# Moving half of a depthwise convolution from VectorE to diagonal matrix products on TensorE, and taking C from the joint projection, in the front part of a state-space and mixture-of-experts kernel

## The chip, the cores and the metric

The kernel runs on one core of one Trainium2 chip. The metric is the device time of one execution, in microseconds (us); lower is better.

## The reference, cut to what matters

```
xn = layernorm(x)                                   # x: 2 x 2048 tokens x 512 channels
xc = depthwise causal convolution of xn, 4 taps per channel, + conv_b
x_conv = silu(xc)
proj = x_conv @ xproj_w.T                           # 512 -> 128 (dt_in) + 16 (B_in) + 16 (C_in)
delta = softplus(dt_in @ dtproj_w.T + dtproj_b)
h_t = exp(delta * A) * h_(t-1) + delta * B_in * x_conv    # scan over time, 16 states per channel
y = sum over the states of h * C_in + xn * D
g = silu(mixture_of_experts(xn))                    # 8 experts, top 2, capacity 1024 each
out = x + y * g
```

## The kernel before, in words

The program has three parts that follow one another: `front`, `main_loop` (the experts' products with the scan woven in) and `tail`. The change touches `front` alone.

`front` works in 8 chunks of 512 tokens (`NCH`, `CH`), with the 512 channels as 4 tiles of 128 partitions (`KT`, written kt). Its first half normalises the chunks, turns them to channels by tokens (`xnT`, each chunk with 3 tokens of the chunk before as a halo) and computes the router's logits. Its second half, which the change is about, does for each chunk ch:

- VectorE, `convolve` (L492 to L507): four taps on each of four channel tiles, from `xnT` into `conv`: one `tensor_scalar` (L502, first tap and bias) and three `scalar_tensor_tensor` (L506) for a tile, 16 instructions a chunk. It waits until the silu of the chunk before has read `conv`.
- ScalarE, `silu` (L349 to L354): four activations from `conv` back into `xnT`.
- TensorE, `project` (L277 to L285): for each kt one product for the 128 dt rows (L283, to `pX` bank 0) and one for the 16 B rows (L284, to bank 1).
- ScalarE, `copy_projection` (L356 to L363): copies dt into `dtin` and B into `brows`; `store_b` sends B to memory.
- TensorE, `widen_dt` (L287 to L293): four products into the four banks of `pT`. Then `c_by_token` (L295 to L303): C by tokens, 4 token blocks times 4 kt, 16 products of 16 columns each with the tokens as stationary operand, into `pC`.
- ScalarE, `softplus` (L370 to L388): reads `pT` into `z`, then Abs, Exp (two halves each) and, after waits for stores and for `u`, Ln. `copy_ct` (L365 to L368) then copies C into `ct`.
- VectorE, `soft` (L574 to L592) and GpSimd (L439): the rest of softplus; L592 writes delta. GpSimd (L445) multiplies delta by the silu's result to `u`. GpSimd also scatters the router's table by 64 indirect DMAs (L434): 24 ahead of chunk 0, then 7 a chunk.
- SyncE stores delta and u and reads the router's table back (L213), for which VectorE waits (L604) ahead of its last `soft`.

Nothing schedules this: each engine runs its own program in the order in which it is written, and semaphores do the rest. ScalarE's loop is, for chunk ch: `copy_projection(ch)`, `silu(ch + 1)`, `store_b(ch)`, `softplus(ch)`, `copy_ct(ch)`. VectorE's is `convolve(ch + 2)`, `soft(ch)`. TensorE's is `project`, `widen_dt`, `c_by_token`. Ahead of its loop VectorE does `convolve(0)` and then some 60 small instructions of the router, at whose end the semaphore `placed` is raised; `pC` holds the router's counts until then. The float32 products are recorded as two instructions each, so counts of matmuls in the trace are twice those of the code.

Of the kernel before, what the change touches and what calls it, by code (L numbers as in the profile page):

```python
# [29 lines left out]
ALU = mybir.AluOpType  # L30
ACT = mybir.ActivationFunctionType
AX = mybir.AxisListType.X
ds = bass.ds

P = 128
B, T, D = 2, 2048, 512
S = B * T
KT = D // P
N = 16
TAPS = 4  # L40
R = 128
E, HID = 8, 2048
CAP = 2 * S // E
CH = 512
NCH = S // CH
CPB = T // CH
TPC = CH // P
# [5 lines left out]
HALO = TAPS - 1  # L53
# [4 lines left out]
C_TAP, C_CONVB, C_DTB, C_ALOG = 0, TAPS, TAPS + 1, TAPS + 2  # L58
# [33 lines left out]
def apart(eng, sem):  # L92

    eng.sem_inc(sem, 1)


def front(nc, a, dr, keep):

    with ExitStack() as ctx:
        sb, psum, sems = memory(nc, ctx)  # L100
        ident, tri, ones = sb("f_ident", [P, P]), sb("f_tri", [P, P]), sb("f_ones", [P, P])
# [15 lines left out]
        lgT = sb("lgT_sb", [E, CH])  # L117
        logits = sb("logits_sb", [P, NT, E])
        zeros, warm = sb("zeros_sb", [P, 512]), sb("f_warm", [P, 1])
        conv = sb("conv_sb", [P, KT, CH])  # L120
        dtin = sb("dtin_sb", [P, CH])
        brows = sb("brows_sb", [N, CH])
        za, z = sb("za_sb", [P, KT, CH]), sb("z_sb", [P, KT, CH])
        ln = sb("ln_sb", [P, KT, CH])
        back = sb("back_sb", [P, KT, CH])
# [14 lines left out]
        pC = psum("pC", [P, 2, CH])  # L140

        s_ = sems("f_", """early consts x_in0 x_in1 xn_out0 xn_out1 cleared stats moments power normed xT xT_copied
            lgT lgT_copied lg lg_copied route shifted exped masks counted placed defaults scattered table
            indexed zeroed halo taps silu proj dtin b_rows b_out dt dt_read absz expz
            lnz rounded dropped dropped_dve soft delta u_done delta_out u_out neg_a ct ct_copied
            pe_at act_at dve_at sp_at pool_at""")

# [75 lines left out]
        @block.tensor  # L223
        def _(pe):
            for name, credits in (("xT", KT + 1), ("lg", 1), ("proj", 1), ("dt", 1)):
                pe.sem_inc(s_[name], credits)
            pe.wait_ge(s_["early"], 16 * len(early))

            def turn(ch, u, i):

                pe.wait_ge(s_["normed"], ch + 3)
                for kt in range(KT):

                    pe.wait_ge(s_["xT_copied"], KT * ch + kt + 1)
                    for j in range(TPC):
                        mm = pe.transpose(pT[:, kt, j * P:(j + 1) * P], xn[:, u, j, kt * P:(kt + 1) * P], ident[:])
                    mm.then_inc(s_["xT"], 1)

            def logits_T(ch):

                pe.wait_ge(s_["xT_copied"], KT * ch + 2 * KT)
                pe.wait_ge(s_["lgT_copied"], ch + 1)
                for kt in range(KT):
                    mm = pe.matmul(pX[0:E, 0, :], wg[:, kt, :], xnT[:, ds(ch, 1), kt, HALO:], start=(kt == 0), stop=(kt == KT - 1))
                mm.then_inc(s_["lgT"], 1)

            def turn_logits(ch):
                pe.wait_ge(s_["lgT_copied"], ch + 2)

                pe.wait_ge(s_["lg_copied"], ch + 1)  # L250
                apart(pe, s_["pe_at"])
                for j in range(TPC):
                    mm = pe.transpose(pX[:, 1, j * E:(j + 1) * E], lgT[:, j * P:(j + 1) * P], ident[0:E, 0:E])
                mm.then_inc(s_["lg"], 1)

            turn(0, 0, 0)
            with pe.Fori(0, NCH // 2 - 1) as i:
                for u in range(2):
                    logits_T(2 * i + u)
                    turn(2 * i + u + 1, 1 - u, i)  # L260
                    turn_logits(2 * i + u)
            logits_T(NCH - 2)
            turn(NCH - 1, 1, 0)
            turn_logits(NCH - 2)
            logits_T(NCH - 1)
            turn_logits(NCH - 1)

            pe.wait_ge(s_["consts"], 16 * len(consts))

            pe.wait_ge(s_["masks"], 1)  # L270
            pe.wait_ge(s_["lg_copied"], NCH + 1)
            for s in range(2):
                for k, w in enumerate((tri, ones)):
                    mm = pe.matmul(pC[:, s, k * NT * E:(k + 1) * NT * E], w[:], mask[s][:].rearrange("p t e -> p (t e)"), start=True, stop=True)
            mm.then_inc(s_["counted"], 1)

            def project(ch):  # L277

                pe.wait_ge(s_["b_rows"], ch + 1)
                for kt in range(KT):  # L280
                    pe.wait_ge(s_["silu"], KT * ch + kt + 2)
                    xs = xnT[:, ds(ch, 1), kt, HALO:]
                    pe.matmul(pX[:, 0, :], xprojT[:, kt, 0:R], xs, start=(kt == 0), stop=(kt == KT - 1))  # L283
                    mm = pe.matmul(pX[0:N, 1, :], xprojT[:, kt, R:R + N], xs, start=(kt == 0), stop=(kt == KT - 1))  # L284
                mm.then_inc(s_["proj"], 1)  # L285

            def widen_dt(ch):  # L287

                pe.wait_ge(s_["dtin"], ch + 1)
                for kt in range(KT):  # L290

                    pe.wait_ge(s_["dt_read"], KT * ch + kt + 1)
                    pe.matmul(pT[:, kt, :], dtprojT[:, kt * P:(kt + 1) * P], dtin[:], start=True, stop=True).then_inc(s_["dt"], 1)  # L293

            def c_by_token(ch):  # L295

                pe.wait_ge(s_["placed"], 1)
                pe.wait_ge(s_["ct_copied"], ch + 1)
                for tb in range(TPC):
                    for kt in range(KT):  # L300
                        xs = xnT[:, ch, kt, HALO + tb * P:HALO + (tb + 1) * P]
                        mm = pe.matmul(pC[:, 0, tb * N:(tb + 1) * N], xs, xprojT[:, kt, R + N:], start=(kt == 0), stop=(kt == KT - 1))
                mm.then_inc(s_["ct"], 1)  # L303

            for ch in range(NCH):
                project(ch)
                widen_dt(ch)
                c_by_token(ch)

        @block.scalar  # L310
        def _(act):
            for name, credits in (("xT_copied", KT), ("lgT_copied", 1), ("lg_copied", 1), ("silu", 1), ("b_rows", 1),
                                  ("dt_read", KT), ("b_out", 16), ("ct_copied", 1)):
                act.sem_inc(s_[name], credits)

# [32 lines left out]

            def silu(ch):  # L349

                for kt in range(KT):
                    act.wait_ge(s_["taps"], KT * (TAPS * ch + HALO) + kt + 1)
                    apart(act, s_["act_at"])
                    act.activation(xnT[:, ds(ch, 1), kt, HALO:], conv[:, kt, :].unsqueeze(1), ACT.Silu).then_inc(s_["silu"], 1)  # L354

            def copy_projection(ch):  # L356
                act.wait_ge(s_["proj"], ch + 2)

                act.wait_ge(s_["dt"], KT * ch + 1)
                act.activation(dtin[:], pX[:, 0, :], ACT.Copy).then_inc(s_["dtin"], 1)  # L360

                act.wait_ge(s_["b_out"], 16 * ch + 16)
                act.activation(brows[:], pX[0:N, 1, :], ACT.Copy).then_inc(s_["b_rows"], 1)  # L363

            def copy_ct(ch):  # L365
                act.wait_ge(s_["ct"], ch + 1)
                apart(act, s_["act_at"])
                act.activation(keep["ct"][:, ds(TPC * ch, TPC), :], pC[:, 0, 0:TPC * N].rearrange("p (j n) -> p j n", n=N), ACT.Copy).then_inc(s_["ct_copied"], 1)  # L368

            def softplus(ch):  # L370

# [17 lines left out]

            def store_b(ch):  # L390

                act.wait_ge(s_["b_rows"], ch + 2)
                act.dma_start(dr.b[ds(ch, 1)].rearrange("o n t -> n (o t)"), brows[:]).then_inc(s_["b_out"], 16)

            silu(0)
            with act.Fori(0, NCH - 1) as ch:
# [51 lines left out]
        def _(dve):  # L448
# [43 lines left out]
            def convolve(ch):  # L492

                dve.wait_ge(s_["silu"], KT * ch + 1)
                for k in range(TAPS):
                    for kt in range(KT):
                        x = xnT[:, ds(ch, 1), kt, HALO - k:HALO - k + CH]
                        c = conv[:, kt, :].unsqueeze(1)
                        tap = chan[:, kt, C_TAP + HALO - k:C_TAP + HALO - k + 1]
                        if k == 0:  # L500

                            op = dve.tensor_scalar(c, x, tap, chan[:, kt, C_CONVB:C_CONVB + 1], ALU.mult, ALU.add)  # L502
                        else:

                            dve.wait_ge(s_["taps"], KT * (TAPS * ch + k - 1) + kt + 1)
                            op = dve.scalar_tensor_tensor(out=c, in0=x, scalar=tap, in1=c, op0=ALU.mult, op1=ALU.add)  # L506
                        op.then_inc(s_["taps"], 1)  # L507

            dve.wait_ge(s_["halo"], 1)
            convolve(0)  # L510
            chain = [0]

            def link(op):
# [775 lines left out]
```

## Time and profile before

| what | us |
|---|---|
| median of 3 runs | 2161.86 |
| lowest and highest run | 2161.03, 2163.65 |
| the profiled execution, its own time | 2175.82 |
| its span | 2174.0 |
| `front` in it (to the first DMA of `main_loop`) | 0 to 307.5 |
| from there until TensorE is done | 307.5 to about 2110 |
| `tail` | about 2110 to 2174.0 |

Times in the rows below are of the profiled execution and count from its span's start. In the timelines a row is a group of like instructions that follow one another: start, time from the first start to the last end, engine, line, operation, output and inputs, count, and in brackets the idle time of the engine ahead of the group and what ended it. A busy TensorE row contains the time that its matmuls take at the clock then granted, which is one of two levels, 1.2 and 2.4 GHz.

### The profile page before, as it was taken

To read this page: it belongs to the slowest core of one execution; us is meant where nothing else is said; L and a number is where in the kernel's file an instruction comes from. 1 tells how busy PE (TensorE), PEld (TensorE's weight loads), DVE (VectorE), ACT (ScalarE), POOL (GpSimd) and SP (SyncE) were. 2 spreads that over 40 slices of the span, in tenths; PEclk is the share of its full clock that TensorE was granted. 3 is DMA by queue.
4 is the path that set the end of the run, shared out by engine and by line. 5 is a ranking of instruction groups with operands and counts; after the bars stand their busy time and mean duration, and the time that the engine had idled before them with its cause. 6 is when DMAs were issued, how large, how long until landed. Compare 5 with 4: busy or idle time off the path is not lost. (4 is left out here: it accounts for less than half of the span.)

```text
span 2174.0 us, 30995 instructions
## 1 busy us (share of the span) xinstructions
PE 1884.3 (87%) x9160; PEld 1477.4 (68%) x9160; DVE 1909.0 (88%) x2038; ACT 1215.3 (56%) x1778; POOL 1383.0 (64%) x606
## 2 busy tenths in 40 slices
PE   6667829999999999999999999999999999999500
PEld 3223317888778788878887888788877887788400
DVE  6777938988998889898989998999899989988599
ACT  3265737656656665656565655665656565655121
POOL 1167748657866676667567756675667566766444
PEclk9877758999999999999999999999999999999855
DMA  9623344214421451235124412441244124321597
GB/s 290 238 44 77 118 187 97 83 58 140 96 80 63 136 117 63 68 128 116 63 68 133 116 58 68 147 102 58 73 142 102 58 79 152 89 75 62 133 320 248
DMA packets 89192, 246.96 MB, mean 114 GB/s; under 512 B 13296, under 2 KB 14320, under 8 KB 77808
## 3 DMA queue, kind: packets, MB, share of 16 engines
q1 hardware_dynamic: 70640, 207.30, 28.2%
q0 software_dynamic: 18176, 37.83, 9.6%
q8 instruction: 72, 1.18, 0.2%
q14 instruction: 48, 0.39, 0.1%
q10 hardware_dynamic: 256, 0.26, 0.1%
HBM read 173.66 MB, written 71.70 MB: 113 GB/s over the span
## 5 line engine op out<-in xcount | busy, mean ns | idle before, releaser
L988 POOL TENSOR_TENSOR ub_sb<-u_sb,brow_sb 128x1024 f32<-128x1024 f32 x256 | 639.7, 2499 | 410.2 <-DVE a_sb L1078 406.3
L1078 DVE TENSOR_TENSOR_SCAN a_sb<-a_sb,state,ub_sb 128x512 f32<-128x512 f32 x512 | 884.5, 1767 | 11.6 <-issue 7.7
L738 PE MATMUL pm<-xTh,w1l 128*128 128x512 f32 x1024 | 424.2, 414 | 11.8 <-DVE xTl L1026 5.3
L738 PE MATMUL pm<-w2h,hl 128*128 128x512 f32 x1024 | 423.9, 414 | 0.0
L740 PE MATMUL pm<-xTh,w1h 128*128 128x512 f32 x1024 | 402.8, 393 | 0.0
L740 PE MATMUL pm<-w2h,hh 128*128 128x512 f32 x1024 | 402.5, 393 | 0.0
L739 PE MATMUL pm<-w2l,hh 128*128 128x512 f32 x1024 | 399.5, 390 | 0.0
L739 PE MATMUL pm<-xTl,w1h 128*128 128x512 f32 x1024 | 399.3, 390 | 0.0
L1049 DVE SCALAR_TENSOR_TENSOR s_acc<-pt,ct_keep,s_acc 128x512 f32<-128x512 f32 x480 | 352.1, 734 | 27.1 <-PE pt L768 26.2
L888 ACT ACTIVATE a_sb<-delta_sb,neg_a_keep 128x512 f32<-128x512 f32 x512 | 330.1, 713 | 6.5
L768 PE MATMUL pt<-m_ident,a_sb 128*128 128x128 f32 x2048 | 308.2, 273 | 25.5 <-DVE a_sb L1078 17.8
L768 PEld LDWEIGHTS pt<-m_ident,a_sb 128*128 128x128 f32 x2048 | 250.6, 139 | 100.4 <-issue 24.0
L911 ACT ACTIVATE hh<-pm,b_keep 128x512 fp32r<-128x512 f32 x256 | 176.1, 688 | 176.3 <-PE pm L740 172.1
L1058 DVE TENSOR_TENSOR hl<-pm,hh 128x512 fp32r<-128x512 f32 x256 | 174.4, 681 | 73.4 <-ACT pm L912 69.4
L738 PEld LDWEIGHTS pm<-xTh,w1l 128*128 128x128 f32 x1024 | 193.6, 189 | 44.4 <-issue 8.3
L740 PEld LDWEIGHTS pm<-xTh,w1h 128*128 128x128 f32 x1024 | 192.8, 188 | 44.0
L740 PEld LDWEIGHTS pm<-w2h,hh 128*128 128x128 f32 x1024 | 192.6, 188 | 43.5
L739 PEld LDWEIGHTS pm<-xTl,w1h 128*128 128x128 f32 x1024 | 194.1, 190 | 32.8
L739 PEld LDWEIGHTS pm<-w2l,hh 128*128 128x128 f32 x1024 | 194.0, 189 | 32.8
L738 PEld LDWEIGHTS pm<-w2h,hl 128*128 128x128 f32 x1024 | 193.4, 189 | 30.8
L977 POOL TENSOR_TENSOR w2l<-w_raw,w2h 128x2048 fp32r<-128x2048 f32 x32 | 176.9, 5527 | 55.2 <-ACT w2h L850 55.2
L1066 DVE SCALAR_TENSOR_TENSOR part<-pm,gate_keep,part 128x512 f32<-128x512 f32 x256 | 186.8, 730 | 27.8 <-PE pm L740 27.8
(130 smaller groups left out, 2139.9 us busy)
## 6 DMA issues: line engine op xcount, KB each, us to landing
w_raw<-in_w SPq DMA_DIRECT2D x64, 1024.0 KB, 5.0
brow_sb<-b_chunks SPq DMA_DIRECT2D x128, 256.0 KB, 3.5
moe_rows<-zeros_sb SPq DMA_DIRECT2D x5, 2048.0 KB, 16.8
xin_sb<-in_x SPq DMA_DIRECT2D x8, 1024.0 KB, 6.3
xn_rows<-xn_sb SPq DMA_DIRECT2D x8, 1024.0 KB, 8.5
delta_chunks<-ln_sb SPq DMA_DIRECT2D x8, 1024.0 KB
u_chunks<-u_now_sb SPq DMA_DIRECT2D x16, 512.0 KB, 4.7
delta_sb<-delta_chunks SPq DMA_DIRECT2D x8, 1024.0 KB, 7.8
```

What stands on the lines that cost most here:

```text
L738: pe.matmul(out, sl, mh, start=start, stop=False)
L739: pe.matmul(out, sh, ml, start=False, stop=False)
L740: return pe.matmul(out, sh, mh, start=False, stop=stop)
L768: mm = pe.transpose(pt[:, bank(s, last), kt * P:(kt + 1) * P], abuf[:, m, kt, tb * P:(tb + 1) * P], ident[:])
L888: op = act.activation(abuf[:, m, kt, :], delta[:, kt, :], ACT.Exp, scale=keep["neg_a"][:].rearrange("p n k -> p (n k)")[:, ds(col, 1)])
L911: act.activation(hh[:, g, j, :], pm[:, j, :], ACT.Gelu, bias=bias)
L977: pool.tensor_tensor(lo[:].rearrange("p k f -> p (k f)"), raw[:], hi[:].rearrange("p k f -> p (k f)").bitcast(F32), ALU.subtract).then_inc ...
L988: pool.tensor_tensor(ub[:, h], u[:, 2 * h:2 * h + 2, :], brow[:, m % 2:m % 2 + 1, :].to_broadcast([P, 2, CH]), ALU.mult).then_inc(s_["bmul ...
L1049: dve.scalar_tensor_tensor(out=acc, in0=h, scalar=c, in1=acc, op0=ALU.mult, op1=ALU.add).then_inc(s_["summed"], 1)
L1058: dve.tensor_tensor(hl[:, g, j, :], pm[:, j, :], hh[:, g, j, :].bitcast(F32), ALU.subtract).then_inc(s_["h_free"], 1)
L1066: dve.scalar_tensor_tensor(out=part[:, t, :], in0=pm[:, t % 4, :], scalar=gate, in1=part[:, t, :], op0=ALU.mult, op1=ALU.add).then_inc(s_[ ...
L1078: op = dve.tensor_tensor_scan(abuf[:, m, 2 * h + k, :], abuf[:, m, 2 * h + k, :], ub[:, h, k, :], state[:, ds(col, 1)], ALU.mult, ALU.add)
```

## The change

Half of the channel tiles (kt 2 and 3) are convolved by TensorE. VectorE builds once, between `convolve(0)` and the router's instructions, 8 diagonal matrices of 128 by 128 from the taps (`diag`). For each chunk TensorE's new `convolve` accumulates four products per tile (a diagonal matrix by `xnT` shifted by one token a tap) in `pC`; silu reads `pC` with the bias of the convolution. C comes with B: the product of L284 now has 32 output rows, `copy_projection` copies all 32 rows, and `turn_c` turns them by four small transposes into bank 1 of `pX`, from which `copy_ct` picks C. As the transposes share that bank with the B and C rows of the next projection, `project` now also waits for `ct_copied`. TensorE's unrolled loop over chunks becomes a loop with register addresses; in it the convolution of chunk ch + 1 stands ahead of the projection of chunk ch.

```diff
-        conv = sb("conv_sb", [P, KT, CH])
+        conv = sb("conv_sb", [P, KT // 2, CH])
+        diag = sb("diag_sb", [P, KT // 2, TAPS, P])
...
-        brows = sb("brows_sb", [N, CH])
+        bcrows = sb("bcrows_sb", [2 * N, CH])
...
+            def convolve(ch):
+
+                pe.wait_ge(s_["silu"], KT * ch + 1)
+                for i, kt in enumerate(range(KT // 2, KT)):
+                    for k in range(TAPS):
+                        mm = pe.matmul(pC[:, i, :], diag[:, i, k, :], xnT[:, ds(ch, 1), kt, HALO - k:HALO - k + CH],
+                                       start=(k == 0), stop=(k == TAPS - 1))
+                    mm.then_inc(s_["conv_pe"], 1)
+
             def project(ch):
 
-                pe.wait_ge(s_["b_rows"], ch + 1)
+                pe.wait_ge(s_["bc_rows"], ch + 1)
+                pe.wait_ge(s_["ct_copied"], ch + 1)
                 for kt in range(KT):
                     pe.wait_ge(s_["silu"], KT * ch + kt + 2)
                     xs = xnT[:, ds(ch, 1), kt, HALO:]
                     pe.matmul(pX[:, 0, :], xprojT[:, kt, 0:R], xs, start=(kt == 0), stop=(kt == KT - 1))
-                    mm = pe.matmul(pX[0:N, 1, :], xprojT[:, kt, R:R + N], xs, start=(kt == 0), stop=(kt == KT - 1))
+                    mm = pe.matmul(pX[0:2 * N, 1, :], xprojT[:, kt, R:], xs, start=(kt == 0), stop=(kt == KT - 1))
                 mm.then_inc(s_["proj"], 1)
...
-            def c_by_token(ch):
-
-                pe.wait_ge(s_["placed"], 1)
-                pe.wait_ge(s_["ct_copied"], ch + 1)
+            def turn_c(ch):
+
+                pe.wait_ge(s_["bc_rows"], ch + 2)
+                apart(pe, s_["pe_at"])
                 for tb in range(TPC):
-                    for kt in range(KT):
-                        xs = xnT[:, ch, kt, HALO + tb * P:HALO + (tb + 1) * P]
-                        mm = pe.matmul(pC[:, 0, tb * N:(tb + 1) * N], xs, xprojT[:, kt, R + N:], start=(kt == 0), stop=(kt == KT - 1))
+                    mm = pe.transpose(pX[:, 1, tb * 2 * N:(tb + 1) * 2 * N], bcrows[:, tb * P:(tb + 1) * P], ident[0:2 * N, 0:2 * N])
                 mm.then_inc(s_["ct"], 1)
 
-            for ch in range(NCH):
+            pe.wait_ge(s_["placed"], 1)
+            pe.wait_ge(s_["diag"], 1)
+            pe.wait_ge(s_["halo"], 1)
+            convolve(0)
+            with pe.Fori(0, NCH - 1) as ch:
+                convolve(ch + 1)
                 project(ch)
                 widen_dt(ch)
-                c_by_token(ch)
+                turn_c(ch)
+            project(NCH - 1)
+            widen_dt(NCH - 1)
+            turn_c(NCH - 1)
...
             def silu(ch):
 
-                for kt in range(KT):
-                    act.wait_ge(s_["taps"], KT * (TAPS * ch + HALO) + kt + 1)
+                for kt in range(KT // 2):
+                    act.wait_ge(s_["taps"], KT // 2 * (TAPS * ch + HALO) + kt + 1)
                     apart(act, s_["act_at"])
                     act.activation(xnT[:, ds(ch, 1), kt, HALO:], conv[:, kt, :].unsqueeze(1), ACT.Silu).then_inc(s_["silu"], 1)
+                for i, kt in enumerate(range(KT // 2, KT)):
+                    act.wait_ge(s_["conv_pe"], KT // 2 * ch + i + 1)
+                    apart(act, s_["act_at"])
+                    act.activation(xnT[:, ds(ch, 1), kt, HALO:], pC[:, i, :].unsqueeze(1), ACT.Silu,
+                                   bias=chan[:, kt, C_CONVB:C_CONVB + 1]).then_inc(s_["silu"], 1)
...
                 for k in range(TAPS):
-                    for kt in range(KT):
+                    for kt in range(KT // 2):
...
             convolve(0)
+            for i in range(KT // 2):
+                for k in range(TAPS):
+                    tap = chan[:, KT // 2 + i, C_TAP + HALO - k:C_TAP + HALO - k + 1]
+                    op = dve.tensor_scalar(diag[:, i, k, :], ident[:], tap, None, ALU.mult)
+            op.then_inc(s_["diag"], 1)
```

TensorE of the kernel before, from the widening of one chunk (L293) over its C (L302) to the projection of the next (L283, L284):

```order
L293 MATMUL pT<-dtin_sb,dtprojT_sb 128x512 [waits f_dt_read,f_dtin]
L293 MATMUL pT<-dtin_sb,dtprojT_sb 128x512 [waits f_dt_read] x3
L302 MATMUL pC<-xprojT_sb,xnT_sb 128x16 [waits f_ct_copied,f_placed]
L302 MATMUL pC<-xprojT_sb,xnT_sb 128x16 x15
L283 MATMUL pX<-xnT_sb,xprojT_sb 128x512 [waits f_silu,f_b_rows]
```

TensorE of the changed kernel, in its loop (its lines are numbered anew: L283 is the convolution, L294 and L295 the projection), from the last product of the convolution of chunk ch + 1 into the projection of chunk ch:

```order
L283 ISA
L283 MATMUL pC<-xnT_sb,diag_sb 128x512
L292 ISA [waits f_ct_copied,f_bc_rows]
L294 ISA [waits f_silu]
L294 MATMUL pX<-xnT_sb,xprojT_sb 128x512
L295 MATMUL pX<-xnT_sb,xprojT_sb 32x512
```

The wait for `ct_copied` has moved from C's product to the head of the projection, and the convolution of the next chunk stands ahead of that wait. Where C's 16 products stood, the changed kernel has, up to the end of the loop's body (L304 is the widening, L311 the turning):

```order
L303 REGISTER_ALU [waits f_dtin]
L304 MATMUL pT<-dtin_sb,dtprojT_sb 128x512 [waits f_dt_read] x4
L308 REGISTER_ALU
L311 MATMUL pX<-f_ident,bcrows_sb 128x32 [waits f_bc_rows]
L311 MATMUL pX<-f_ident,bcrows_sb 128x32 x3
L318 REGISTER_ALU
L318 COMPARE_AND_BRANCH
```

Four transposes stand in the place of the 16 products, and they wait for the copied rows.

## Rows read from the trace of the kernel before

**Rows 1.** Busy time by stage: front, main loop; length, engines, PEclk, DMA share, GB/s
```profile
0.00:307.50 307.50, 200.76 (x680) 88.23 (x680) 224.73 (x347) 153.80 (x250) 149.79 (x108) 0.81 0.48 149
307.50:2110.00 1802.50, 1683.53 (x8480) 1389.16 (x8480) 1624.42 (x1647) 1050.46 (x1518) 1205.43 (x490) 0.97 0.35 102
```
**Rows 2.** Timeline of VectorE, one round of its loop (L502 to L592)
```profile
193.46 5.83 DVE L502 TENSOR_SCALAR conv_sb<-xnT_sb,chan_sb 128x512 f32 x4
199.20 8.02 DVE L506 SCALAR_TENSOR_TENSOR conv_sb<-xnT_sb,chan_sb,conv_sb 128x512 f32<-128x512 f32 x12
207.15 1.33 DVE L580 TENSOR_SCALAR back_sb<-za_sb 128x1024 f32<-128x1024 f32 x2
...
214.22 2.36 DVE L592 TENSOR_TENSOR ln_sb<-ln_sb,back_sb 128x1024 f32<-128x1024 f32 x2
```
**Rows 3.** Timeline of GpSimd, from chunk 1 to chunk 3
```profile
164.51 13.45 POOL L445 TENSOR_TENSOR u_now_sb<-ln_sb,xnT_sb 128x1024 f32<-128x1024 f32 x2 [8.53 <-DMA u_chunks<-u_now_sb]
...
187.53 2.36 POOL L439 TENSOR_TENSOR back_sb<-za_sb,back_sb 128x1024 f32<-128x1024 f32 x1
192.55 5.35 POOL L445 TENSOR_TENSOR u_now_sb<-ln_sb,xnT_sb 128x1024 f32<-128x1024 f32 x2 [2.66 <-DVE ln_sb L592]
198.06 1.00 POOL L434 DMA_INDIRECT slot_table<-entry_sb,place_sb  x1 [0.16 <-issue]
...
206.38 1.02 POOL L434 DMA_INDIRECT slot_table<-entry_sb,place_sb  x1 [0.31 <-issue]
```
**Rows 4.** Timeline of ScalarE: copy of dt, silu; and, a chunk later, softplus to C's copy
```profile
229.04 0.60 ACT L360 ACTIVATE dtin_sb<-pX 128x512 f32<-128x512 f32 x1 [1.75 <-PE pX L284]
...
231.05 1.13 ACT L354 ACTIVATE xnT_sb<-conv_sb 128x512 f32 x2
...
260.32 1.26 ACT L377 ACTIVATE z_sb<-pT,chan_sb 128x512 f32<-128x512 f32 x2 [5.70 <-DVE back_sb L587]
...
269.69 2.00 ACT L388 ACTIVATE ln_sb<-za_sb 128x1024 f32<-128x1024 f32 x2
271.60 0.20 ACT L368 ACTIVATE ct_keep<-pC 128x64 f32 x1
```
**Rows 5.** Timeline of TensorE: small transposes, widening, C, projection
```profile
66.14 0.41 PE L253 MATMUL pX<-f_ident,lgT_sb 8*128 8x8 f32 x4
...
98.55 3.70 PE L293 MATMUL pT<-dtin_sb,dtprojT_sb 128*128 128x512 f32 x8 [0.78 <-ACT dtin_sb L360]
102.09 3.64 PE L302 MATMUL pC<-xprojT_sb,xnT_sb 128*128 128x16 f32 x32
108.68 2.05 PE L283 MATMUL pX<-xnT_sb,xprojT_sb 128*128 128x512 f32 x2 [2.95 <-ACT xnT_sb L354]
...
118.38 1.03 PE L284 MATMUL pX<-xnT_sb,xprojT_sb 128*16 128x512 f32 x2
124.18 5.40 PE L293 MATMUL pT<-dtin_sb,dtprojT_sb 128*128 128x512 f32 x8 [4.78 <-issue]
...
132.91 1.11 PE L283 MATMUL pX<-xnT_sb,xprojT_sb 128*128 128x512 f32 x2
...
140.00 1.03 PE L284 MATMUL pX<-xnT_sb,xprojT_sb 128*16 128x512 f32 x2
```
**Rows 6.** Timelines, the first convolution and the end of the router's chain (VectorE)
```profile
68.02 1.91 DVE L502 TENSOR_SCALAR conv_sb<-xnT_sb,chan_sb 128x512 f32<-128x512 f32 x4 [0.42 <-DVE xnT_sb L489]
69.85 8.03 DVE L506 SCALAR_TENSOR_TENSOR conv_sb<-xnT_sb,chan_sb,conv_sb 128x512 f32<-128x512 f32 x12
...
99.26 0.18 DVE L569 CAST place_sb<-c 128x32 int32<-128x32 f32 x1
```
**Rows 7.** Timelines, the last chunk: ScalarE, VectorE, GpSimd
```profile
273.22 0.60 ACT L360 ACTIVATE dtin_sb<-pX 128x512 f32<-128x512 f32 x1 [1.43 <-PE pX L284]
...
288.07 0.17 DVE L604 CAST add_row_keep<-vacant_sb 128x8 int32<-128x8 f32 x1 [8.30 <-DMA filled_sb<-slot_table]
...
296.88 5.14 POOL L445 TENSOR_TENSOR u_now_sb<-ln_sb,xnT_sb 128x1024 f32<-128x1024 f32 x2 [4.88 <-DVE ln_sb L592]
```

More of the change, by code:

```diff
@@ L142, in front @@
         s_ = sems("f_", """early consts x_in0 x_in1 xn_out0 xn_out1 cleared stats moments power normed xT xT_copied
-            lgT lgT_copied lg lg_copied route shifted exped masks counted placed defaults scattered table
-            indexed zeroed halo taps silu proj dtin b_rows b_out dt dt_read absz expz
+            lgT lgT_copied lg lg_copied route shifted exped diag conv_pe masks counted placed defaults scattered table
+            indexed zeroed halo taps silu proj dtin bc_rows b_out dt dt_read absz expz
             lnz rounded dropped dropped_dve soft delta u_done delta_out u_out neg_a ct ct_copied
@@ L293, in widen_dt @@
                     pe.matmul(pT[:, kt, :], dtprojT[:, kt * P:(kt + 1) * P], dtin[:], start=True, stop=True).then_inc(s_["dt"], 1)
-            def c_by_token(ch):
-                pe.wait_ge(s_["placed"], 1)
-                pe.wait_ge(s_["ct_copied"], ch + 1)
+            def turn_c(ch):
+                pe.wait_ge(s_["bc_rows"], ch + 2)
+                apart(pe, s_["pe_at"])
                 for tb in range(TPC):
-                    for kt in range(KT):
-                        xs = xnT[:, ch, kt, HALO + tb * P:HALO + (tb + 1) * P]
-                        mm = pe.matmul(pC[:, 0, tb * N:(tb + 1) * N], xs, xprojT[:, kt, R + N:], start=(kt == 0), stop=(kt == KT - 1))
+                    mm = pe.transpose(pX[:, 1, tb * 2 * N:(tb + 1) * 2 * N], bcrows[:, tb * P:(tb + 1) * P], ident[0:2 * N, 0:2 * N])
                 mm.then_inc(s_["ct"], 1)
-            for ch in range(NCH):
+            pe.wait_ge(s_["placed"], 1)
[4 more added lines that the diff above has]
+                convolve(ch + 1)
                 project(ch)
                 widen_dt(ch)
-                c_by_token(ch)
+                turn_c(ch)
+            project(NCH - 1)
+            widen_dt(NCH - 1)
+            turn_c(NCH - 1)
         @block.scalar
         def _(act):
-            for name, credits in (("xT_copied", KT), ("lgT_copied", 1), ("lg_copied", 1), ("silu", 1), ("b_rows", 1),
+            for name, credits in (("xT_copied", KT), ("lgT_copied", 1), ("lg_copied", 1), ("silu", 1), ("bc_rows", 1),
                                   ("dt_read", KT), ("b_out", 16), ("ct_copied", 1)):
@@ L362, in copy_projection @@
                 act.wait_ge(s_["b_out"], 16 * ch + 16)
-                act.activation(brows[:], pX[0:N, 1, :], ACT.Copy).then_inc(s_["b_rows"], 1)
+                act.activation(bcrows[:], pX[0:2 * N, 1, :], ACT.Copy).then_inc(s_["bc_rows"], 1)
             def copy_ct(ch):
@@ L367, in copy_ct @@
                 apart(act, s_["act_at"])
-                act.activation(keep["ct"][:, ds(TPC * ch, TPC), :], pC[:, 0, 0:TPC * N].rearrange("p (j n) -> p j n", n=N), ACT.Copy).then_inc(s_["ct_copied"], 1)
+                act.activation(keep["ct"][:, ds(TPC * ch, TPC), :], pX[:, 1, 0:TPC * 2 * N].rearrange("p (j n) -> p j n", n=2 * N)[:, :, N:], ACT.Copy).then_inc(s_["ct_copied"], 1)
             def softplus(ch):
@@ L390, in store_b @@
             def store_b(ch):
-                act.wait_ge(s_["b_rows"], ch + 2)
-                act.dma_start(dr.b[ds(ch, 1)].rearrange("o n t -> n (o t)"), brows[:]).then_inc(s_["b_out"], 16)
+                act.wait_ge(s_["bc_rows"], ch + 2)
+                act.dma_start(dr.b[ds(ch, 1)].rearrange("o n t -> n (o t)"), bcrows[0:N, :]).then_inc(s_["b_out"], 16)
             silu(0)
@@ L503, in convolve @@
                         else:
-                            dve.wait_ge(s_["taps"], KT * (TAPS * ch + k - 1) + kt + 1)
+                            dve.wait_ge(s_["taps"], KT // 2 * (TAPS * ch + k - 1) + kt + 1)
                             op = dve.scalar_tensor_tensor(out=c, in0=x, scalar=tap, in1=c, op0=ALU.mult, op1=ALU.add)
```

## The prediction

> **What bounds the kernel now.** I read the stages first: the change touches `front` alone, 307.5 of 2174 us; what follows starts when `front` is over, and its work is the same [rows 1]. So I ask only when `front` ends.
>
> Within `front` I read the timelines of the four engines side by side. VectorE's round (the four first taps, the other twelve, then `soft`) runs without a gap from 193.46 to 216.58, 23.1 us [rows 2]. Of that the convolution is 13.7 (to 207.15) and `soft` 9.4. The first taps took 5.83 there for four and 1.91 where GpSimd was still [rows 2, 6]: GpSimd's L445 ran from 192.55, beside them [rows 3]. The Trainium skill (SBUF — State Buffer, "Who interferes with whom") says that such instructions of the two engines shut each other out, whole instructions at a time; the trace agrees, and goes beyond it, since one pair of L445 took 13.45 us where the next took 5.35.
>
> ScalarE in the same rounds waits: 5.70 us for VectorE's L587 ahead of softplus [rows 4]. TensorE waits too, 4.78 and 2.95 us in two places [rows 5]. So the round is VectorE's, and the change halves the convolution on it. The question is which loop comes next.
>
> **The wait that decides.** In the changed program `project(ch + 1)` waits for `ct_copied` of chunk ch, ScalarE's last act in softplus, and ScalarE's next act, the copy of dt, waits for that projection. Before, only C's product waited for that copy, so a projection could run beside softplus. Now ScalarE and TensorE take turns in one closed loop. Its price, from the rows:
>
> - start of the copy of dt to the end of silu: 229.04 to 232.18, 3.14; with the step to the first read of `pT` I take 3.2 [rows 4]. The widening is ready by then: its first of four products needs about 0.9 of the 3.70 [rows 5].
> - softplus to the end of C's copy, no waits in it: 260.32 to 271.80, 11.5 [rows 4]
> - the step to TensorE: 0.1
> - the projection: 132.91 to 141.03, 8.1 [rows 5]; 32 output rows in place of 16 stream the same 512 columns, so I add nothing. Ends: 0 and, were the second product to lose what the wider load takes, well under 0.1 each, 0.4 a chunk.
> - the step back to ScalarE: 0.15
>
> Sum **23.05 us**, the same as VectorE's round of 23.1. The work taken off VectorE is hidden behind a new wait of the same length.
>
> **The other parts, costed.**
>
> - VectorE loses 8 of 16 instructions a chunk: half of 1.91 + 8.03 is 4.9, and up to 2 more where the first taps collided [rows 2, 6]. Its round falls to 16 to 18 us, beside the new loop: worth nothing.
> - GpSimd's own round: L439, the wait for L592, L445 and seven scatters, 187.53 to 207.40, 19.9 us [rows 3]. Under 23.05, so hidden; margin 3. `soft` starts no later in the loop than before relative to its Exp, so SyncE's stores of delta and u, the same ones, keep their place.
> - TensorE gains the convolution: 8 products, 16 recorded instructions, of the shape of the widening, 8 of which took 3.70; so 7.2 at the high clock [rows 5]. It loses C, 3.64, and gains four transposes, 0.41 for four small ones, up to twice that for 32 columns: 0.8 [rows 5]. They fit in the loop: from the start of the copy of dt, 0.65 to the widening, 3.7, 0.8, 7.2 make 12.4, against 14.7 when C is copied. TensorE then stands still for **2.4 us** ahead of each projection, 7 times.
> - silu from `pC`: 4 activations as before; I take no difference. A loop with registers in place of an unrolled one: the logits' loop in the first half already has that form, nothing.
> - The start: VectorE's `convolve(0)` shrinks by 4.9; the 8 diagonals cost between 0.18 (128 x 32) and 0.48 (a quarter of 1.91, 512 wide) each; I take 0.2, as 128 is nearer to 32 wide, 1.6 in all (ends 1.4 and 3.8) [rows 6]. `placed` moves from 99.4 to 96.1. But TensorE's `convolve(0)` now stands behind `placed` where the first projection did not: it starts at 96.2 after a long pause, at the low clock, 7.2 + 1.7 (the widening after a pause took 5.40 instead of 3.70 [rows 5]) to 105.1; silu to 105.7; `convolve(1)` to 112.9; `project(0)` to 121.0; copy of dt at **121.2**.
> - Seven rounds of 23.05: the last copy of dt at 282.6, against 273.22 before [rows 7].
> - The end: no silu in the last round, so softplus starts 1.7 after the copy; Exp is done 8.1 later; VectorE's steps from there to the end of the first L592 are `soft`'s 9.4 less half of L580's 1.33 and half of L592's 2.36, 7.6, and less what it stood there beside GpSimd's L439, at most its 2.36, so 5.2 [rows 2, 3]; L439 starts some 3 us ahead of the second Exp's end and is out of the way, so I take 5.5; GpSimd 5.14 [rows 7]. Together 20.5. Last u at **303.1**, against 302.0 before. The 8.30 us that VectorE waited for the router's table ahead of its last `soft` [rows 7] are gone in that: the last scatter is issued one round and a half before. What is late in its place is the projection.
>
> Sum at the high clock: **+1.1 us**.
>
> **The clock.** After 2.95 us of standing still the projection started at the low clock: the first two instructions took 2.05 against 1.11, and the whole 108.68 to 119.41, 10.7 against 8.1 [rows 5]. After 0.78 us the widening ran at the high one (3.70), after 4.78 it started low (5.40). The Trainium skill (TensorE: Matmul & The Clock Gate, "What's actually happening") says that activity releases the clock and rest throttles it; the trace agrees. The new pause of 2.4 us is nearest to the 2.95. What speaks against the same fall: ahead of the 2.95 stood C's narrow products, ahead of the new pause full ones. Every fall costs 2.6 on the loop's path (10.7 less 8.1). Ends: none of 7, 0; all of 7, 18. I take half: **+9**.
>
> Total +10. On the profiled execution's own 2175.82 that is 2186; the runs without the profiler lie 14 lower, and I apply the difference to their median: 2161.86 + 10 = **2172 us**. A measurement of this kernel tells changes of over 0.2%, 4.3 us, from none.
>
> **The rivals.**
>
> 1. *The clock holds* in all or all but one of the pauses, since wide products precede them: +1 to +4, **no change**. For it: 0.78 us did no harm; against it: the 2.95.
> 2. *GpSimd's round becomes the bound*, **faster**. If the loop of ScalarE and TensorE were no tie, the round would fall from 23.05 to the 19.9 of rows 3, seven times 3.2 is 22: +1 - 22 = -21, 2141 us. It decides as soon as projection and softplus overlap by more than 3.2 us. For it: VectorE has no gap today [rows 2] and loses 4.9 and its collisions. Against it: the order printed above, in which the wait for `ct_copied` stands ahead of the projection. By the skill's page on SBUF alone, the engine that is shut out less would give that time back; here the time is real (13.45 against 5.35) but no longer on the path.
> 3. *The low clock stays*: the rows at the low clock are 1.85 times as long (2.05 against 1.11 [rows 5]); TensorE's round of 8.1 + 3.7 + 7.2 becomes 35.2, with 1.6 of transposes and step 36.8, and TensorE is the bound: seven times 13.7, +96, 2259 us. Against it: both long projections in rows 5 end at the high clock.
> 4. *GpSimd is shut out once more* by VectorE, as at 164.51 [rows 3]: 13.45 less 5.35 is 8 on top of the forecast, 2180 us. Against it: VectorE now rests several us in each round, which lets GpSimd in.
>
> **How the numbers follow.** Forecast (+4.3 to +20): 0.67. Rival 1: 0.17. Rival 2: 0.08. Rival 3: 0.03. Rival 4: 0.05. Faster is rival 2, 0.08; same is rival 1, 0.17; slower the rest, 0.75. The range leaves out rivals 2 and 3 and the tips of the forecast: from 2160 (no fall, and 3 less on the start and steps) to 2184 (+22: all seven falls, diagonals and steps at their upper ends).
>
> **What would show it.** Right: TensorE's rows ahead of the projection (L294) read 2 to 3 us idle, released by ScalarE's copy of C; copies of dt 23 to 26 us apart, the first near 121; VectorE idle 5 us or more a round; granted clock of the convolution rows mostly high, the projection's first rows mixed; no wait at the table. Wrong: copies of dt under 21 us apart (rival 2), or the projection released by silu and not by C's copy, or convolution rows of over 12 us (rival 3).

## The result, and the profile after

The changed kernel takes **2188.44 us** (median; 2188.19 to 2189.44), the kernel before on the same chip 2161.66 (2161.03 to 2163.65). The ratio is 1.0123 (95% interval 1.0106 to 1.0141): slower by 26.8 us, where 10 were forecast, in a range that ended at 2184. The profiled execution of the changed kernel took 2189.44, with a span of 2187.6.

Busy time by stage of the changed kernel, columns as in [rows 1]; `front` is over at 324.27, where it was at 307.58 in the profiled execution of before:

```profile
0.00:324.00 324.00, 224.20 (x584) 80.10 (x584) 161.11 (x291) 154.17 (x250) 134.18 (x108) 0.88 0.40 142
324.00:2126.00 1802.00, 1682.64 (x8480) 1388.42 (x8480) 1634.48 (x1647) 1052.48 (x1520) 1206.31 (x490) 0.97 0.35 103
```

The main loop is the same, and `front` has grown although VectorE works 64 us less in it (224.73 to 161.11). The chain is the one forecast. Timeline of TensorE, chunks 2 and 3, and the first convolution:

```profile
95.85 9.14 PE L283 MATMUL pC<-xnT_sb,diag_sb 128*128 128x512 f32 x16 [10.09 <-DVEq L597]
...
161.32 2.05 PE L294 MATMUL pX<-xnT_sb,xprojT_sb 128*128 x2 [3.11 <-ACT ct_keep L390]
163.30 1.76 PE L295 MATMUL pX<-xnT_sb,xprojT_sb 128*32 x2
165.00 1.12 PE L294 MATMUL pX<-xnT_sb,xprojT_sb 128*128 x2
...
172.01 3.69 PE L304 MATMUL pT<-dtin_sb,dtprojT_sb 128*128 128x512 f32 x8 [0.85 <-ACT dtin_sb L382]
175.64 0.43 PE L311 MATMUL pX<-f_ident,bcrows_sb 32*128 32x32 f32 x4
176.00 7.13 PE L283 MATMUL pC<-xnT_sb,diag_sb 128*128 x16
186.24 2.07 PE L294 MATMUL pX<-xnT_sb,xprojT_sb 128*128 x2 [3.10 <-ACT ct_keep L390]
188.24 1.92 PE L295 MATMUL pX<-xnT_sb,xprojT_sb 128*32 x2
190.08 2.08 PE L294 MATMUL pX<-xnT_sb,xprojT_sb 128*128 x2
192.09 1.05 PE L295 MATMUL pX<-xnT_sb,xprojT_sb 128*32 x2
```

TensorE has done the next chunk's convolution at 183.1 and stands for 3.1 us until ScalarE has copied C. The two projections shown then run at the low clock for their first four or six recorded instructions of 16, and take 9.8 and 11.0 us in place of 8.1. ScalarE's side of the same loop, answering to [rows 4], and the last copy of dt:

```profile
171.29 0.60 ACT L382 ACTIVATE dtin_sb<-pX 128x512 f32<-128x512 f32 x1 [8.81 <-PE pX L295]
...
174.43 1.23 ACT L399 ACTIVATE z_sb<-pT,chan_sb 128x512 f32<-128x512 f32 x2
...
185.68 0.20 ACT L390 ACTIVATE ct_keep<-pX 128x64 f32 x1
...
197.32 0.60 ACT L382 ACTIVATE dtin_sb<-pX 128x512 f32<-128x512 f32 x1 [9.93 <-PE pX L295]
...
297.64 0.60 ACT L382 ACTIVATE dtin_sb<-pX 128x512 f32<-128x512 f32 x1 [9.82 <-PE pX L295]
```

The first copy of dt is at 121.46 and the last at 297.64: seven rounds of 25.17 on the mean. VectorE, in the same stretch, and its last `soft`, against [rows 2, 7]:

```profile
174.69 1.00 DVE L524 TENSOR_SCALAR conv_sb<-xnT_sb,chan_sb 128x512 f32 x2 [10.30 <-ACT xnT_sb L375]
175.61 4.06 DVE L528 SCALAR_TENSOR_TENSOR conv_sb<-xnT_sb,chan_sb,conv_sb 128x512 f32<-128x512 f32 x6
...
291.09 2.14 DVE L631 CAST add_row_keep<-vacant_sb 128x8 int32<-128x8 f32 x1
...
304.49 0.69 DVE L607 TENSOR_SCALAR back_sb<-za_sb 128x1024 f32<-128x1024 f32 x1 [8.90 <-ACT za_sb L403]
```

Its convolution takes 5.0 us, where it took 13.7 in the round of [rows 2] and 9.9 without a collision [rows 6]. It waits 10.30 in the round instead, released by ScalarE. The wait of 8.30 for the router's table is gone (L631 follows at once), and 8.90 for the last chunk's Exp stand in its place.

### The profile page after: what moved, and what is told of

The parts are those of the page before. It is cut to its first block and busy times, and to the rows that moved or that the text cites. A ratio compares the mean times of both kernels' runs of the same rounds, so it can differ in the third digit from the quotient of the medians.

```text
span 2187.6 us, 30806 instructions
## 1 busy us (share of the span) xinstructions
PE 1906.8 (87%) x9064; PEld 1468.5 (67%) x9064; DVE 1853.0 (85%) x1982; ACT 1215.8 (56%) x1778; POOL 1366.5 (62%) x606
## 6 DMA issues: line engine op xcount, KB each, us to landing
moe_rows<-zeros_sb SPq DMA_DIRECT2D x5, 2048.0 KB, 16.8
```

## The experiments

Times in each are set against runs of the kernel before on the same chip. "Over" is where `front` ends in a profile, the first DMA of `main_loop`.

### The kernel before, twice more

The profiled execution of before took 2175.82, its runs 2161. The forecast had put the 14 us down to the profiler. This run is the unchanged kernel.

> The kernel before, unchanged, for a second profile. Theory A (the first profiled execution of it was 14 us longer than its runs because GpSimd was shut out once, L445 with 13.45 us at 164.51, and VectorE waited 8.30 us for the router's table): a profiled execution near 2162, front over near 293 instead of 307.5, no L445 pair above 8 us. Theory B (the profiler adds 14 us to this kernel): 2175 again, and the same 13.45.

Measured: 2162.18, span 2160.4. Timeline of GpSimd, where [rows 3] have the pair of 13.45; and the end of `front`:

```profile
135.32 5.33 POOL L445 TENSOR_TENSOR u_now_sb<-ln_sb,xnT_sb 128x1024 f32<-128x1024 f32 x2 [2.67 <-issue]
...
158.33 5.35 POOL L445 TENSOR_TENSOR u_now_sb<-ln_sb,xnT_sb 128x1024 f32<-128x1024 f32 x2 [4.88 <-DVE ln_sb L592]
...
181.36 5.34 POOL L445 TENSOR_TENSOR u_now_sb<-ln_sb,xnT_sb 128x1024 f32<-128x1024 f32 x2 [4.88 <-DVE ln_sb L592]
...
285.94 5.14 POOL L445 TENSOR_TENSOR u_now_sb<-ln_sb,xnT_sb 128x1024 f32<-128x1024 f32 x2 [4.88 <-DVE ln_sb L592]
...
296.64 0.35 SPq L671 DMA_DIRECT2D m_ident<-in_ident  x1
```

There is no long pair, and `front` is over at 296.64, 10.9 before the first profile's 307.58. A third profile of the kernel before gave the same.

> The kernel before, unchanged, a third profile, to see how often L445 is shut out. Theory A (an event of single executions, not of the profiler): near 2162 with no L445 pair above 8 us, or near 2168 to 2176 with one. Theory B (the first profile is typical): 2175 with the pair of 13.45.

Measured: 2165.7, over at 296.07, again no pair above 5.34. So the profiler does not cost 14 us. The first profiled execution of before was an unusual one. Against 296.64 the changed `front` is over 27.6 us later, and 26.8 is what the runs show.

One thing has to be kept apart in such comparisons. The small transposes of [rows 5], in the first half of `front`, which no edit touches, start at 63.66 here and at 65.79 in the profile of the changed kernel. Both values turn up with both kernels: 63.6 to 63.9 in five of the thirteen profiles, 65.6 to 66.1 in the other eight. So a difference of about 2 us between two ends of `front` can lie ahead of everything that was changed; "like start" below means that it is taken off.

### C's copy taken forward

The theory: the loop of ScalarE and TensorE is the loss, and it exists because the projection waits for ScalarE's last act in softplus. The edit puts `copy_ct` between the halves of softplus, the same work in another place:

```diff
                     act.activation(za[:, h], za[:, h], ACT.Exp, scale=-1.0).then_inc(s_["expz"], 1)
+                    if h.start == 0:
+                        copy_ct(ch)
...
                 softplus(ch)
-                copy_ct(ch)
```

> The changed kernel with one edit: C is copied between the two halves of softplus, so the projection no longer waits for the end of softplus. If the closed loop of ScalarE and TensorE is the cause: the pause ahead of each projection goes, the round falls from 25.2 to 20.5 (TensorE: 0.85 + 3.7 + 0.4 + 7.1 + 8.2 + 0.2), seven rounds give back 33, about 2155 us, below the kernel before. If the convolution on TensorE itself is too dear: no round under 23, 2175 or more.

Measured: 2155.4 (2152.93 to 2157.54), ratio 0.9961 (0.9947 to 0.9976), over at 288.31. Against the changed kernel's 2188.44 that is 33 us less (34 at the end of `front`, from a like start). Its timeline of TensorE, and of VectorE in the same round:

```profile
204.21 7.13 PE L283 MATMUL pC<-xnT_sb,diag_sb 128*128 x16
211.19 1.02 PE L294 MATMUL pX<-xnT_sb,xprojT_sb 128*128 x2
...
218.24 1.04 PE L295 MATMUL pX<-xnT_sb,xprojT_sb 128*32 x2
220.13 3.69 PE L304 MATMUL pT<-dtin_sb,dtprojT_sb 128*128 128x512 f32 x8 [0.85 <-ACT dtin_sb L382]
```

```profile
219.11 1.22 DVE L614 SCALAR_TENSOR_TENSOR back_sb<-z_sb,back_sb 128x1024 f32<-128x1024 f32 x1 [4.50 <-POOL back_sb L461]
```

The projection follows the convolution without a pause, at the high clock. Copies of dt are 19.9 us apart, and TensorE stands for only 0.85 us a round: it bounds them. GpSimd's first six pairs of L467 are 20.5 to 21.8 apart, so GpSimd falls behind TensorE by 5.6 us over these five rounds. It bounds when u is ready, and VectorE waits 4.50 for it. The wait for the table is back, 8.10 us at 268.80.

### The pause filled

Is the low clock a matter of the pause, and what is it worth? TensorE does three products more behind each convolution, into a bank of `pT` that is free by then. They are extra work whose result is overwritten.

```diff
                 convolve(ch + 1)
+                pe.wait_ge(s_["dt_read"], KT * ch + 1)
+                for _ in range(3):
+                    pe.matmul(pT[:, 0, :], diag[:, 0, 0, :], xnT[:, ds(ch + 1, 1), KT // 2, HALO:], start=True, stop=True)
                 project(ch)
```

> The changed kernel with three products of no use (2.7 us at the high clock) behind each convolution in the loop; their result is overwritten. If the low clock after the pause is what rounds of 25.2 have over 23.2: six pauses shrink below 0.5 us, the projections behind them take 8.2, rounds of 23.2, and the first round pays 2.7 for work where there was no pause: 9 us less, 2179. If the clock falls all the same or the rounds are long for another reason: 2188 to 2204.

Measured: 2182.24 (2178.9 to 2184.36), ratio 1.0078 (1.0057 to 1.0099), over at 316.43. TensorE's timeline:

```profile
182.58 2.74 PE L322 MATMUL pT<-xnT_sb,diag_sb 128*128 x6
185.95 1.12 PE L294 MATMUL pX<-xnT_sb,xprojT_sb 128*128 x2 [0.63 <-ACT ct_keep L393]
187.00 1.05 PE L295 MATMUL pX<-xnT_sb,xprojT_sb 128*32 x2
```

After 0.63 us of rest the projection starts at the high clock, and the copies of dt are 23.28 us apart, where the forecast had summed 23.05. The last projection, with no convolution ahead of it, still has 9.99 us of rest and a low start. More work on TensorE made the kernel faster (by 6 us between the medians, 8 at the end of `front`), and it is still slower than before: the clock is part of the loss. The rest is the closed loop, most of it in the last two rounds (47.7 us between GpSimd's products, 35.6 in before), and the later start.

### C's part alone

The kernel before, with only C's new path and its wait; the convolution stays on VectorE.

```diff
             def project(ch):
...
+                pe.wait_ge(s_["ct_copied"], ch + 1)
...
-                    mm = pe.matmul(pX[0:N, 1, :], xprojT[:, kt, R:R + N], xs, start=(kt == 0), stop=(kt == KT - 1))
+                    mm = pe.matmul(pX[0:2 * N, 1, :], xprojT[:, kt, R:], xs, start=(kt == 0), stop=(kt == KT - 1))
...
+                    mm = pe.transpose(pX[:, 1, tb * 2 * N:(tb + 1) * 2 * N], brows[:, tb * P:(tb + 1) * P], ident[0:2 * N, 0:2 * N])
```

> The kernel before with only the C part of the change (joint product of 32 rows, four transposes, the projection waits for C's copy); all of the convolution stays on VectorE. If the new wait is the cause: rounds of 25.5 to 26 with pauses of 9 to 10 us ahead of the projections, 2172 to 2184. If the convolution on TensorE is what costs: 2162, as before.

Measured: 2180.45 (2177.74 to 2180.97), ratio 1.007 (1.005 to 1.0091), over at 312.20, copies of dt 24.4 to 25.7 apart from the third on. TensorE's timeline:

```profile
121.79 2.04 PE L284 MATMUL pX<-xnT_sb,xprojT_sb 128*128 128x512 f32 x2 [19.75 <-ACT ct_keep L367]
...
199.45 2.05 PE L284 MATMUL pX<-xnT_sb,xprojT_sb 128*128 128x512 f32 x2 [9.89 <-issue]
```

With the whole convolution on VectorE the loop is about as long as with half of it. C's part alone brings more than half of the loss: 18 of 27 us between the medians, 13.5 of 25.5 at the end of `front` from a like start.

### C's part with the early copy, the convolution on VectorE

This is the run above with `copy_ct` between the halves: does the first experiment's gain come from C's path or from the convolution?

> The C part of the change alone, with the early copy of C, all of the convolution on VectorE. VectorE's round of 23.0 should bound it again: 2161 to 2164, like the kernel before; then the 7 us that the early copy with half the convolution on TensorE gains are the convolution's. If C's part gains by itself (TensorE loses 3.6 us of C a chunk): 2158 or less.

Measured: 2161.2 (2157.94 to 2163.91), ratio 0.9986 (0.9976 to 0.9995), over at 296.43, GpSimd's first six pairs 23.0 us apart, as in the kernel before. C's path costs nothing once its copy is early. It may even gain a little: 2.7 us between the medians, an interval that just leaves out 1, and 2 us at the end of `front` from a like start. The rest of the early copy's 7 to 8 us, some 4 to 6, belongs to the convolution.

### A quarter of the convolution, C as before

The kernel before, with one of the four tiles on TensorE, into `pC[:, 1]`, and no new wait ahead of the projection.

```diff
+            def convolve(ch):
+                pe.wait_ge(s_["silu"], KT * ch + 1)
+                for k in range(TAPS):
+                    mm = pe.matmul(pC[:, 1, :], diag[:, k, :], xnT[:, ds(ch, 1), KT - 1, HALO - k:HALO - k + CH],
+                                   start=(k == 0), stop=(k == TAPS - 1))
```

> The kernel before with one of four channel tiles convolved by TensorE into the free bank of pC and C as before, so no closed loop. If moving work off VectorE is worth what its instructions cost as long as no new wait takes its place: rounds of 20.5 to 21 (VectorE 20.3, TensorE 20, GpSimd 19.9), the first copy of dt near 114, about 2150 us. If the convolution on TensorE hurts by itself: 2162 or more.

Measured: 2154.2 (2150.57 to 2155.36), ratio 0.996 (0.9946 to 0.9974), over at 289.64, copies of dt 21.2 us apart on the mean. That is 4 us above the forecast of 2150, and the rounds are a little longer than the 20.5 to 21 expected. A quarter, without touching C, gains what half does with the early copy.

### Why one profile of before was long

Theory: in that execution GpSimd came late to L445 (its wait for the last store of u ended at 164.51), after VectorE had begun the twelve second taps (the two-input instructions of L506), and was shut out until they were over. Why that store landed so late no run shows. Rival: anything else that is slow once. The first edit holds GpSimd back once, in chunk 1.

```diff
+                if ch == 1:
+                    pool.wait_ge(s_["delta"], 2 * ch + 3)
+                    pool.memset(late[:], 0.0)
```

> The kernel before, but in chunk 1 GpSimd waits for the second half of delta and clears a buffer nobody reads before its first L445, so that it comes some 2 us late, behind the start of VectorE's convolution. If a late GpSimd is shut out until that convolution ends: an L445 pair of 11 to 14 us in chunk 1 and a later end by 8 us or more, 2168 to 2176. If the lateness costs only itself: 2162 to 2165.

Measured: 2164.27 (2160.43 to 2167.95), ratio 1.0002 (0.9991 to 1.0013). The edit missed its aim. VectorE's first taps ran from 158.97, and GpSimd came in among them:

```profile
160.37 4.66 POOL L449 TENSOR_TENSOR u_now_sb<-ln_sb,xnT_sb 128x1024 f32<-128x1024 f32 x2
```

The pair was short, and VectorE's four first taps took 6.34, where they take 5.81 to 5.83 in the kernel's other rounds. So it tests nothing of the second taps. The second edit waits until one second tap is done:

```diff
+                if ch == 1:
+                    pool.wait_ge(s_["taps"], KT * TAPS * (ch + 3) + KT + 1)
```

> The kernel before, but in chunk 1 GpSimd's first L445 waits until VectorE has done the fifth of its 16 convolution instructions, so that it comes into the run of two-input ones (about 4 us later than it would). If GpSimd is shut out for that whole run: an L445 pair of 11 to 14 us in chunk 1, the next copy of dt 8 us late and front longer by 6 to 9 us, about 2170. If it gets in between two instructions: a pair of 6 us and no more than 4 us on the end.

Measured: 2173.27 (2171.27 to 2174.59), ratio 1.0041 (1.0027 to 1.0056), over at 305.63. Its timelines of GpSimd and of VectorE:

```profile
163.92 13.50 POOL L447 TENSOR_TENSOR u_now_sb<-ln_sb,xnT_sb 128x1024 f32<-128x1024 f32 x2 [8.49 <-DVE conv_sb L508]
```

```profile
163.04 8.04 DVE L508 SCALAR_TENSOR_TENSOR conv_sb<-xnT_sb,chan_sb,conv_sb 128x512 f32<-128x512 f32 x12
170.99 1.29 DVE L582 TENSOR_SCALAR back_sb<-za_sb 128x1024 f32<-128x1024 f32 x2
172.32 3.07 DVE L586 TENSOR_TENSOR back_sb<-za_sb,back_sb 128x1024 f32<-128x1024 f32 x1
175.43 3.07 DVE L589 SCALAR_TENSOR_TENSOR back_sb<-z_sb,back_sb 128x1024 f32<-128x1024 f32 x1
```

The pair of 13.45 of [rows 3] is there again as 13.50: its first instruction takes 10.39, the second 3.15. `front` ends 9 us later than at 296.6, 7 from a like start, and the medians are 8.8 apart. VectorE's twelve taps lose nothing (8.04, where [rows 6] have 8.03) while GpSimd is shut out. This is shown: one late arrival costs the kernel 7 to 9 us.

### Two attempts to go further

The first adds to the early copy an earlier table: VectorE does its last `soft` ahead of the wait for the table, and SyncE stores chunk 6 before it waits for the scatters.

```diff
-            with sp.Fori(0, NCH - AHEAD) as ch:
+            with sp.Fori(0, NCH - 1) as ch:
...
+            soft(NCH - 1)
...
-            soft(NCH - 1)
```

> The kernel with the early copy of C, and two edits at the end of front: VectorE does its last soft before it waits for the router's table, and SyncE stores chunk 6 before it waits for the scatters. Its wait of 8.1 us for the table then stands behind soft. If that wait is on the path: 3 to 5 us less than the early copy alone, near 2151. If the stores or ScalarE are late next: within 1 us of 2155.

Measured: 2153.43 (2151.81 to 2160.35), ratio 0.9952 (0.9936 to 0.9968), over at 288.29 against 288.31 without it. The wait has gone from VectorE. The end of `front` is the same to 0.02 us, but this execution began its second half 2.2 us later (66.04 against 63.85 for the small transposes), so from a like start the edit gained 2 us, and 2.0 is also what lies between the medians. The two intervals overlap: the gain is not clear of noise. One of GpSimd's products now waits 4.44 us at 247.38 for a store of u, and the table's copies run beside the last one (2.14 and 2.16 us in place of 0.17 and 0.19). The second lets GpSimd do L461's subtraction ahead of its scatters:

```diff
+                if ch:
+                    pool.wait_ge(s_["rounded"], 2 * ch + 1)
+                    pool.tensor_tensor(back[:, HALVES[0]], za[:, HALVES[0]], back[:, HALVES[0]], ALU.subtract).then_inc(s_["dropped"], 1)
```

> The kernel with the early copy of C, and GpSimd does L439 of a chunk ahead of its seven scatters instead of behind them (from chunk 1 on). There GpSimd and TensorE both make rounds of 19.9, and VectorE waits 4.5 us for L439 in each. If GpSimd sets the rounds of 20.5 to 21.2 seen in its L445 rows: they fall to TensorE's 19.9, 3 to 6 us less, near 2151. If TensorE alone sets them: no difference, 2155.

Measured: 2170.15 (2163.22 to 2176.01), ratio 1.0029 (1.0016 to 1.0042), over at 303.64. It is 15 us slower than the early copy alone, which neither theory had. GpSimd's products now fall into VectorE's convolution, whose timeline reads:

```profile
210.98 8.46 DVE L532 SCALAR_TENSOR_TENSOR conv_sb<-xnT_sb,chan_sb,conv_sb 128x512 f32<-128x512 f32 x6
```

That is six taps in 8.46 us where they took 4.06; the round after it has 8.45. VectorE's wait for the router's table is 13.18 us at 284.11, where the early copy had 8.10. The collision is one part of the loss; the rest of the 15 us was not taken apart.

## Why the prediction failed where it did

**The decisive wait was right.** The projection waits for ScalarE's copy of C, C's copy ends softplus, and the work taken off VectorE is worth nothing behind it: the run with C's part alone loses 0.7%, and taking the copy forward turns +1.23% into -0.39%. The first copy of dt was forecast at 121.2 and came at 121.46. From the last copy of dt to the start of the last L467 15.4 was forecast (20.5 less 5.14) and 15.93 measured. The projection (8.1), the widening (3.69) and the convolution (7.13 against 7.2) are at the high clock what was said; 8 diagonals took 1.65 (1.6).

**The step that failed is the last one: "the runs without the profiler lie 14 lower, I apply the difference to their median".** By its own time the changed kernel was forecast at 2186, and its profiled execution took 2189.44. But 11 of the 14 us lay in `front` and were no cost of the profiler (the other 3 lie behind it, where the second and the third profile of before differ by 4 as well). Some 8 of them were the pair of 13.45 in [rows 3] (2.5 more lay ahead of the loop: the first copy of dt at 97.90 against 95.38), which I had read, priced at 8, and put into a rival as something that could come once more; that it lay in the base, and in no ordinary run of it, I did not see. The kernel to compare with ends `front` at 296.6. On that base +10 from 307.5 is +21 from 296.6. The seven rounds show it: in the first profile of before they took 175.3 us (97.90 to 273.22), in the second 165.1 (95.38 to 260.48), and it is against the first that I set 7 x 23.05. Rival 4 is thus the wrong way round. The changed kernel had no such pair (all of L467 5.14 to 5.18), and the kernel before had it in one profile of three. Of the 16.8 us by which the forecast was short, some 11 come from this step and 6.7 from what follows here (less 1 behind `front`); either alone would have left the time inside the range, at 2183 or 2179.

**The second step, smaller, is "the clock: I take half, +9".** All seven projections after a rest had low rows (six from the first row on, one, at 136.41, from the second). Six rests were 3.1 us, not 2.4: the turn of C took 0.43, with 0.36 from its start to the next row, where I had 0.8, and the steps were a little longer. The seventh, ahead of the last projection, was 9.9, since no convolution stands there: an oversight. The round without a fall is 23.28 (pause filled), so of seven rounds of 25.17 the falls are 7 x 1.89 = 13.2, against 9, and the high-clock round adds 7 x 0.23 = 1.6. The two together are 5.8 more than forecast; with 0.3 at the first copy of dt and 0.5 behind the last one it is the 6.7 by which `front` ended later than 317.6. My upper end for the clock, 18, was too high: the seven projections took 9.7 to 11.1 against 8.1, so a fall costs 1.6 to 3.0, as the low clock lasts for about four or about six recorded instructions. The size of the pause may have decided: rests of 2.07 and 2.53 us ahead of the widening left the clock high in the two later profiles of before, so at 2.4 it might have held. No run has a pause of 2.4 ahead of the projection.

The page that I had cited (the Trainium skill, TensorE: Matmul & The Clock Gate, "What's actually happening") says that activity releases the clock, and the filled pause agrees: six recorded instructions of no use kept it high, six times of six. Rest was not the only thing ahead of a fall, though: the last section has falls with no rest at all.

**Where the 27.6 us lie** (against the second profile of before). The first u starts at 138.52, not 135.32: +3.2, the start, of which 2.1 lie in the first half, ahead of everything that was changed. From there to the sixth, 126.9 in place of 115.1: +11.8, five longer rounds. The last two rounds take 48.2 in place of 35.6: +12.6. There VectorE had no convolution left and ran ahead in before (17.2 and 18.4 apart); the closed loop has the projection still in it.

**The rivals.** Rival 2 came in the form it named, though not in this kernel: with projection and softplus overlapping, the round is 19.9, `front` is over at 288.3, and -21 from 307.5 would be 286.5. What it is worth to the median is not 21 but 7 to 8 us, mostly by the same wrong base. The rule of the Trainium skill that it weighed (SBUF — State Buffer, "Who interferes with whom"), whole instructions shut out, is borne out by the run with GpSimd held into the taps, with more: the first of GpSimd's two instructions stayed out for the rest of a run of twelve (10.39 us where 3.0 is usual), not for one. Rival 1 is out, by seven falls of seven. Rival 3 is out too; every projection ended at the high clock.

## What to carry to other kernels

Before a difference is added to a median, look at the profiled execution of the base beside its runs: where it is longer than they are, find the row that is long in it, and take it out of the base. When work is taken off the busiest engine, write down the loop that the new waits close, and look at what the waited-for step stands behind in its own queue; here moving one copy of 0.20 us was worth 33 us. The fastest versions are the change with the early copy (0.9961, and 0.9952 with the table's order as well) and a quarter of the convolution with C left alone (0.996); their intervals overlap, and the last is the smallest edit.

## What the hardware did that I had not expected

- GpSimd's two-input product, arriving after VectorE's second taps have begun, is shut out until all twelve are over (13.50 us for two where 5.34 is usual); arriving among the four first taps it gets in, and VectorE pays: 6.34 us where 1.91 is what they take alone and 5.82 beside GpSimd's pair in an ordinary round, and GpSimd's pair 4.66. Why the taps of six in the last experiment let it in (8.46 against 4.06) isn't settled.
- In the changed kernel 3.1 us of rest between full-width products was followed by the low clock each of six times, once only from the third recorded instruction on. Rests of up to 2.53 between products of 512 columns never were, in the second half of `front` of any profile (1.28 ahead of the second convolution; 2.07, 2.23 and 2.53 ahead of the widening in profiles of the kernel before and of the run with GpSimd held into the taps). Between 3.1 and 3.5 both happened: 3.09 us ahead of a widening in the run with GpSimd held into the taps, and 3.27 ahead of the last projection with the early copy, left the clock high, and the same 3.27 with the table's order did not. What decides there is open, and so is why the low clock lasted for four recorded instructions at 161.32 and for six at 186.24, 1.1 us apart.
- A fall needs no rest. Behind C's 16-column products, with nothing between, the first profile of before has the projection at 236.72 start low (1.76 and 1.89 against 1.11 and 1.03), and the quarter's convolutions took 5.38 to 6.59 in four rounds, where 3.70 is the high clock's. Lines of the early copy, and of the quarter:

```profile
247.35 1.10 PE L294 MATMUL pX<-xnT_sb,xprojT_sb 128*128 128x512 f32 x2 [3.27 <-issue]
```

```profile
162.25 3.64 PE L311 MATMUL pC<-xprojT_sb,xnT_sb 128*128 128x16 f32 x32
165.74 5.38 PE L282 MATMUL pC<-xnT_sb,diag_sb 128*128 128x512 f32 x8
```

- The first convolution, after 10.09 us of rest, took 9.14 in place of 7.13: a low start costs 2.0 there, in the size of the 1.7 that the widening had shown.
